# Second edge pass of a graph network kernel: where TensorE turns the weighted rows, and what ScalarE's copy of them waits for

## The reference

```python
x_src = node_feat[edge_src]                                    # [E, 64]
tp    = (x_src[:, :, None] * edge_sh[:, None, :]).reshape(E, 64 * 8)
out1  = concatenate([x_src, tp], -1)                           # [E, 576]
out2  = gelu(gelu(edge_inv @ Wv1) @ Wv2) @ Wv3                 # [E, 576]
edge_v   = out1 * out2 * sqrt(relu(alpha))     # alpha per head: 4 groups of 144 columns
node_out = segment_sum(edge_v, edge_dst)
x = x + node_out @ W_out                                       # [N, 64]
```

## Time and profile before

| | |
|---|---|
| Median of the runs | 4112.56 us |
| Profiled execution, its own time | 4116.36 us |
| Its span | 4114.6 us |
| DVE busy | 3721.7 us (90%) |
| PE busy / weight loads | 3048.8 us (74%) / 1954.9 us (48%) |
| POOL busy / ACT busy | 1859.6 us (45%) / 1777.1 us (43%) |
| Three DVE products of the pass (L1907, L1899, L1913) | 494.8 + 494.7 + 83.9 us |

### The profile page before, as it was taken

The page is one execution under the profiler, slowest core; times in us unless marked ns, Lnnn a source line. Parts: engine busy times, 40 slices in busy tenths (PEclk is TensorE's granted clock), DMA queues, the critical chain, the costliest instruction groups (busy, mean ns, idle before and its releaser), DMA issues. The chain is left out here.

```text
span 4114.6 us, 146181 instructions
## 1 busy us (share of the span) xinstructions
PE 3048.8 (74%) x61717; PEld 1954.9 (48%) x61717; DVE 3721.7 (90%) x5487; ACT 1777.1 (43%) x3388; POOL 1859.6 (45%) x3678
## 2 busy tenths in 40 slices
PE   5666565466469998999992799999999994186166
PEld 2111111221146666666661688888888883123122
DVE  8999999799878988988889899999999995997898
ACT  6999988477423333333331222222222220184085
POOL 0100455200177777777771577777777774000000
PEclk9899988577789999999996899999999996598599
DMA  4763899866345555555551233333333332464554
GB/s 166 301 272 149 287 352 354 293 210 210 100 133 153 156 157 157 154 155 158 156 151 37 79 108 106 105 107 108 105 109 106 106 109 89 172 230 159 195 189 177
DMA packets 412860, 681.16 MB, mean 166 GB/s; under 512 B 75245, under 2 KB 353069, under 8 KB 400561
## 3 DMA queue, kind: packets, MB, share of 16 engines
q1 hardware_dynamic: 336736, 559.22, 41.1%
q0 software_dynamic: 39568, 78.78, 7.1%
q10 hardware_dynamic: 35904, 33.79, 2.8%
HBM read 399.92 MB, written 271.65 MB: 163 GB/s over the span
## 5 line engine op out<-in xcount | busy, mean ns | idle before, releaser
L729 POOL DMA_INDIRECT arena<-h_table,srci x808 | 773.9, 958 | 246.3 <-issue 231.4
L823 PE MATMUL banks<-arena 128*128 128x500 bf16 x1440 | 427.2, 430 | 281.3 <-DVE arena L1496 227.0
L1907 DVE TENSOR_TENSOR arena<-banks,arena 128x1024 f32<-128x1024 f32 x404 | 494.8, 1225 | 43.2 <-PE banks L1048 13.1
L1899 DVE TENSOR_TENSOR arena<-banks,arena 128x1024 f32<-128x1024 f32 x404 | 494.7, 1224 | 38.8 <-ACT arena L1340 10.2
L1785 DVE TENSOR_TENSOR arena<-banks,arena 128x1024 f32<-128x1024 f32 x404 | 492.3, 1219 | 39.0 <-PE banks L930 34.4
L1180 ACT ACTIVATE arena<-arena,h 128x128 bf16<-128x128 f16 x1440 | 454.9, 387 | 83.0 <-DVE arena L1509 43.3
L1048 PE MATMUL banks<-arena 64*64 64x256 f32 x6464 | 439.4, 383 | 9.2 <-DVE arena L1907 1.9
L1067 PE MATMUL banks<-arena 64*64 64x128 f32 x12928 | 438.9, 269 | 5.3 <-issue 4.5
L941 PE MATMUL banks<-arena 64*64 64x128 f32 x12928 | 426.9, 270 | 0.0
L1484 DVE TENSOR_SCALAR arena<-arena,agg 128x500 bf16<-128x500 f16 x1440 | 409.8, 349 | 0.2
L1067 PEld LDWEIGHTS banks<-arena 64*64 64x64 f32 x12928 | 389.5, 133 | 31.9 <-issue 9.3
(11 more groups left out here) (294 smaller groups left out, 5807.5 us busy)
## 6 DMA issues: line engine op xcount, KB each, us to landing
arena<-c_flat SPq DMA_DIRECT2D x75, 1562.5 KB, 6.9
slots<-arena SPq DMA_DIRECT2D x90, 1000.0 KB, 4.3
arena<-hs_dump SPq DMA_DIRECT2D x404, 128.0 KB
arena<-mask_rows SPq DMA_DIRECT2D x50, 781.2 KB, 4.3
arena<-in_edge_attr SPq DMA_DIRECT2D x202, 128.0 KB
arena<-placed SPq DMA_DIRECT2D x202, 128.0 KB
xs_dump<-arena SPq DMA_DIRECT2D x202, 128.0 KB
hs_dump<-arena SPq DMA_DIRECT2D x202, 128.0 KB
```

The source lines that it names most:

```text
L729: pool.indirect_dma_start(out=xs[t % NX][:, k * D:(k + 1) * D], out_offset=None, in_=h_table, in_offset=bass.IndirectOffsetOnAxis(ap=srci[ ...
L823: last = pe.matmul(ps[4 + r % 2][:, 0:BW], row_hot[r][:, k * P:(k + 1) * P], col_hot[r][:, k * BW:(k + 1) * BW], start=k == 0, stop=k == K ...
L1899: V.tensor_tensor(dt_[h].rearrange("p (s n) -> p s n", s=4), banks[:, 0:2 * COLS].rearrange("p (s n) -> p s n", s=4), xat[t % 3].rearrange ...
L1907: V.tensor_tensor(vt[h], banks[:, 2 * COLS:4 * COLS], dt_[h], ALU.mult).then_inc(vt_sb, 1)
```

## The change

PE turns the weighted rows of the next tile ahead of value(t, 1) and no longer behind it. ACT's copy of them no longer waits for the messages that are turned back; these in turn wait, on PE, until the copy is done, since both lie in banks 6 and 7. back(t - 1) asks for t + 2 copies, which is the copy of turned(t + 1); for the last tile it asks for all T.

```diff
@@ PE
             def p2_back(t):
 
                 pe.wait_ge(msg_sb, t + 1)
+                pe.wait_ge(xat_sb, min(t + 3, T))
                 for r in range(2):
...
                 if 0 <= t < T:
                     p2_basis(t, 1)
-                    p2_value(t, 1)
                 if t + 1 < T:
                     p2_turned(t + 1)
+                if 0 <= t < T:
+                    p2_value(t, 1)
                 if 0 <= t - 1:
                     p2_back(t - 1)
@@ ACT
             def p2_turned(t, r):
 
                 act.wait_ge(xa_ps, t + 1)
-                at(msgx_ps, t - 1, act)
                 at(vt_sb, t * 3 - 6, act)
```

## The result

The changed kernel takes 4165.4 us (median of 4 runs, 4164.56 to 4166.49), the one before 4109.8 us (4 runs, 4106.69 to 4118.84): 1.0132 times as long, with an interval of 1.0114 to 1.0149. The forecast was 4086 us, in a range of 4064 to 4111. It is 79 us off and on the wrong side.

The account below looks back on a forecast made before the run. A closed DVE, PE and ACT chain was taken to set 5.50 us a tile; 5.36 after saves 0.14 x 202 = 28 us: 4116.4 to 4088.4, median 4084.6, taken as 4086 us, range 4064 to 4111.

Parts of the forecast that it names:

- The bound of before: Second edge pass: a closed chain through DVE, PE and ACT sets 5.50 us a tile; DVE's floor is 5.09 us.
- The chain of 5.50 us: DVE's values, PE's value(t, 1), turn and back, ACT's copies, PE's own and next value: sum 5.50 us a tile.
- Rival (a): DVE is the limit already: period stays 5.48 to 5.50 us, time 4108 to 4113 us; chance 11%.
- the reading by occupancy: Skill rule: DVE busy 93 stands above TensorE's weight loads 81, so reordering TensorE wins nothing of the steady period.
- The copy no longer waits for back, the turn ahead of value: Cuts the chain; the turn fills PE's 0.30 us wait; steady tile 5.50 to 5.36 us, 28 us gained over 202.
- Both old waits: PE's waits in each tile: 0.30 us before value(t, 1) for DVE, 0.19 us before own for ACT's copy.
- The wait of back: New wait on PE for ACT's copy ahead of back, every tile: 0.30 us, bounds 0 and 0.5.
- Disturbances: About 21 us of the pass above quiet tiles, arising on PE; change set at zero, 10 us to either side.
- (b): Hidden-layer loads become PE's wait: period 5.60 us at a landing time of 4.1 us, time 4133 us; chance 7%.
- (d): Back's wait takes 0.5 us, not 0.3, so PE stands as long as before: period 5.51, time 4113 us; chance 5%.

Follow-up runs that it names:

- e4: Kernel before, with hidden layer and harmonics loaded for the first two tiles only and reused (values wrong): 4102.4 us, ratio 0.9961 to before.
- e9: Changed kernel with only the turn ahead made in whole 128 x 128 tiles, 4 transposes for 32 matmuls: 4075.6 us, ratio 0.9922 to before.
- e2: Kernel before, order kept, but back waits for ACT's copy and the copy no longer for back: 4271.2 us, ratio 1.0374 to before.
- e1: Changed kernel with the turn still moved ahead, but the copy waits for back again and back for no copy: 4125.0 us, ratio 1.0015 to before.
- e11: Kernel before with the turn only moved ahead and made in whole tiles; the copy still waits for back: 4096.8 us, ratio 0.9976 to before.
- e8: Kernel before with 20 always satisfied waits added on PE ahead of value(t, 1): 4167.4 us, ratio 1.0148 to before.

## Why the prediction was wrong

**The bound of before: right.** The chain of 5.50 us was the period of quiet tiles (e4: 5.509), and DVE was not at its limit (5.40 in e9). Rival (a) falls, and with it the reading by occupancy.

**The copy no longer waits for back, the turn ahead of value: right in the quiet tile.** Both old waits are gone, ACT's copy is released by L1084, and a quiet tile takes 5.1 to 5.3 us (median 5.23), even below the 5.36 forecast.

**The wait of back: right in place, a little small.** 0.35 us against 0.30.

**"Disturbances ... I set the balance at zero, with 10 us to either side": this step failed.** I took 21 us of the pass for slips whose sum a reordering leaves alone, though I named "instructions that come late" among them and reasoned that "a late PE stays late". They were for the most part ends of instruction blocks. Before, PE stood still 0.49 us of each tile at two semaphores, and in that time the next block caught up; 52 + 28 us of waits per 1000 us hid most of the supply. With the waits gone PE ran into the blocks. The term that I had set at zero, with 10 us to either side, measured 80 us: the time at block ends went from 38 to 117 us. Against it stands what a quiet tile gained, (5.495 - 5.23) x 201 = 53 us. That makes the pass 26 us longer; measured are 38, so 12 us of this sum are open. That the supply is the cause is shown from three sides: with longer waits (e2), fewer other DMAs (e4) or fewer instructions (e9) the stops go, and in e9 the same change wins.

**The range was too narrow for the same reason.** It had no case in which PE itself can't be fed. None of the named rivals was it: (b) and (d) gave 4133 and 4113 us.

**Open.** Why back's wait brings 23 us more at block ends where blocks are late (changed against e1), while where they are not the same swap wins 0.11 us a tile (e9 against e11). By the DMA records the block's transfer starts a median 88 loads ahead of the block's end in the kernel before, 77 in e1 and 70 in the changed one: with that wait the transfer starts later in the stream. What sets that point I have not shown. Nor have I located more than 38 of the 56 us.

## What to carry to other kernels

Before a wait is taken from an engine that runs many short instructions, look at its time put down to "issue" in the midst of groups, and count the instructions between such stops. If the count is constant, instructions already arrive late now and then, and the wait may be what gives them time. Then make the instructions fewer before you make the order tighter; here 352 to 296 a tile turned a loss of 56 us into a gain of 32. And a set of small irregular delays that all arise on one engine is a mechanism to be named, not noise to be carried over unchanged.

## What the runs showed of the hardware that I had not expected

- PE's instructions come in blocks of 16.4 KB, 256 instructions each (some 126 pairs of load and matmul), and in the changed kernel none is worked on sooner than 2.1 us after its transfer started. At 5.23 us for 352 loads and matmuls most block ends stop PE, by up to 1.5 us.
- Other DMA traffic makes more of these stops: with loads of 304 KB a tile taken away, 46 of them became 16 in the one kernel and 175 became 133 in the other. The blocks' transfers started sooner; they were not shorter.
- Between 64 x 64 and 128 x 128 tiles PE loses 0.39 us behind matmuls of 256 columns in fp32, and 0.17 to 0.20 us at the other three places, in each of 179 tiles.
- A wait that is already satisfied costs PE time: 20 of them, nine instructions in the trace, follow each other at 0.106 us and made each tile 0.25 us longer (e8).
